# Expert choice sums its tokens with the choice as the stationary operand; key jobs, loads and sums of the distance attention in another order

## The reference, cut to what matters

```python
logits = jnp.einsum('bsd,de->bse', x, gate_w) + gate_b      # 32 experts
probs = jax.nn.softmax(logits, axis=-2)                     # over the tokens
vals, idx = top_k(probs, 8)                                 # 8 tokens of each expert and batch
merged = jnp.einsum('bked,bke->bed', tok, vals)             # their weighted sum, one row per expert
h = jax.nn.gelu(concat([merged, 1]) @ w1)                   # 257 x 1024 weights for each expert
o = concat([h, 1]) @ w2
out = scatter of o * vals to the chosen tokens
```

## Time and profile before

| | |
|---|---|
| median of 3 runs | 3237.09 us (3235.47 to 3243.7) |
| profiled execution: own time, span | 3209.46 us, 3207.6 us |
| PE busy | 2754.4 us, 86% of the span |
| DVE, ACT, POOL busy | 1873.4, 1721.7, 850.3 us |
| mean granted TensorE clock | 0.937 |
| expert choice, layer norm to the last sum | 1303.1 to 1528.5 us |
| opening of the layer 2 attention begins | 1529.3 us |
| opening of the layer 3 attention | 2319.5 to 2393.3 us |

### The profile page before, as it was taken

One profiled execution on the slowest core, in us unless ns is written; L12 is line 12 of the kernel. 1 busy time (PEld: TensorE's weight loads), 2 busy tenths in 40 slices (PEclk: granted clock), 3 DMA queues, 4 the chain that ended last, 5 costly groups with the idle time before them and its releaser, 6 DMA issues. The chain is left out here.

```text
span 3207.6 us, 46066 instructions
## 1 busy us (share of the span) xinstructions
PE 2754.4 (86%) x14806; PEld 1548.2 (48%) x14900; DVE 1873.4 (58%) x4757; ACT 1721.7 (54%) x2884; POOL 850.3 (27%) x957
## 2 busy tenths in 40 slices
PE   7899869959999999676699978999857888888887
PEld 3233249924444444432322247999633454444453
DVE  6677551155555555332688740111559999999953
ACT  3566522146555555111277732333149999999953
POOL 4101020030000000021300022000438888888840
PEclk8899989979999999788799999999978999999988
DMA  5111146510000000597212145999340000000011
GB/s 166 53 46 56 43 173 226 200 60 1 1 1 1 1 1 1 217 417 314 80 50 62 46 153 199 342 346 345 110 143 11 20 27 21 23 15 21 18 33 46
DMA packets 162662, 327.86 MB, mean 102 GB/s; under 512 B 29616, under 2 KB 129072, under 8 KB 139056
## 3 DMA queue, kind: packets, MB, share of 16 engines
q1 hardware_dynamic: 152976, 305.63, 27.4%
q0 software_dynamic: 4608, 12.59, 1.2%
q10 hardware_dynamic: 4896, 7.35, 0.7%
HBM read 276.08 MB, written 49.28 MB: 101 GB/s over the span
## 5 line engine op out<-in xcount | busy, mean ns | idle before, releaser
L3164 DVE TENSOR_TENSOR_SCAN L3x_behind<-L3x_first_exp,L3x_beside_scan 128x513 f32<-128x513 f32 x256 | 309.1, 1207 | 0.0
L3044 POOL TENSOR_TENSOR L3x_fade<-L3x_behind,L3x_apart 128x1024 f32<-128x1024 f32 x128 | 280.8, 2193 | 68.5 <-DVE L3x_behind L3164 44.9
L1334 ACT ACTIVATE L1x_probs<-L1x_scores,L1x_neg_max 128x512 f32<-128x512 f32 x256 | 173.5, 683 | 218.7 <-DVE L1x_neg_max L1386 218.7
L1386 DVE TENSOR_REDUCE L1x_neg_max<-L1x_scores 128x2 f32<-128x1024 f32 x128 | 156.5, 1223 | 144.0 <-PE L1x_scores L1234 144.0
L3082 ACT ACTIVATE L3x_first_exp<-L3x_scores,L3x_nm 128x512 f32<-128x512 f32 x256 | 231.6, 905 | 9.8 <-DVE L3x_nm L3156 9.7
L3110 ACT ACTIVATE L3x_probs_T<-L3x_probs_tp 128x512 f32<-128x512 f32 x256 | 207.0, 809 | 12.8 <-PE L3x_probs_tp L2972 12.8
L1667 ACT ACTIVATE L2f_hiddenT<-L2f_hidden_ps,L2f_b1s 128x128 f32<-128x128 f32 x320 | 99.8, 363 | 211.2 <-PE L2f_hidden_ps L1602 211.2
L806 DVE CUSTOM_DVE_ANT_0 L0x_masked_scores<-L0x_s,L0x_mask_q 128x512 f32<-128x512 f32 x256 | 167.0, 685 | 61.7 <-issue 55.8
L3090 ACT ACTIVATE L3x_fade<-L3x_fade,L3x_rl 128x512 f32<-128x512 f32 x256 | 200.5, 955 | 0.0
L801 DVE TENSOR_REDUCE L2x_neg_max<-L2x_s 128x1 f32<-128x512 f32 x256 | 164.6, 685 | 43.2 <-PE L2x_s L697 43.0
L3156 DVE TENSOR_REDUCE L3x_nm<-L3x_scores 128x1 f32<-128x512 f32 x256 | 172.6, 674 | 18.8 <-remote 17.1
(11 more groups left out here) (545 smaller groups left out, 6228.7 us busy)
## 6 DMA issues: line engine op xcount, KB each, us to landing
L2f_w1s<-in_L_w SPq DMA_DIRECT2D x40, 1024.0 KB, 7.7
L2f_w2s<-in_L_w SPq DMA_DIRECT2D x40, 1024.0 KB, 6.4
L1f_w1s<-in_L_w SPq DMA_DIRECT2D x32, 1024.0 KB, 15.4
L1f_w2s<-in_L_w SPq DMA_DIRECT2D x32, 1024.0 KB, 12.9
L0f_w1s<-in_L_w SPq DMA_DIRECT2D x16, 1024.0 KB, 6.1
L0f_w2s<-in_L_w SPq DMA_DIRECT2D x16, 1024.0 KB, 5.2
L0x_q_stack<-L0x_q_parts SPq DMA_DIRECT2D x96, 64.0 KB, 2.6
L0x_k_stack<-L0x_k_parts SPq DMA_DIRECT2D x96, 64.0 KB, 2.7
```

The source lines that it names most:

```text
L1334: nc.scalar.activation(p[:, n % 3, h, :], s[:, n % 2, h, :], ACT.Exp, bias=nmax[:, n % 4, h:h + 1], accum_out=den[:, n % 4, h:h + 1]).then ...
L3044: nc.gpsimd.tensor_tensor(fz[:, f:f + 2, :], bs[:, fb:fb + 2, 0:S], w, ALU.mult).then_inc(y_done, 1)
L3164: nc.vector.tensor_tensor_scan(bs[:, f, :], ex[:, t, :], beside[:, 0:1].to_broadcast([P, S + 1]), 0.0, ALU.add, ALU.bypass).then_inc(f_don ...
```

## The change

1. The sum of the chosen tokens has its operands exchanged: 32 columns of `selT` are stationary and 256 columns of the normed tokens move past, with the four batches in four groups of 32 output partitions. That makes 16 matmuls, a copy of the 128 x 256 result to SBUF, two transposes on PE and the two copies into `expert_tokens`.
2. The key jobs are spread anew. Groups 0 to 4 stay as they are. Group 5 has jobs 9 (between `up` and `turn`), 10 and 11, group 6 jobs 12, 13 and 14 in the same way, and group 7 only job 15, between `up` and `turn`. SP stores jobs 7, 8 and 9 in its turn 6, jobs 10, 11 and 12 in turn 7, and three at the end.
3. In an opening with keys made, ACT waits for the weights before its own loads, and a q job waits only for the two copies of its batch.
4. In the opening of layer 3, SP loads mask, gamma and distance at once after the weights. The sigmoids move to copies 1 to 4, the exponentials to copies 5 and 6 and jobs 1 and 3, the mask's terms and maxima ahead of the jobs on DVE, POOL's product ahead of its jobs, DVE's products to jobs 2, 4 and 6, and the sums of the values behind all jobs.

```diff
@@ norm_and_project, SP, PE
+                if beside:
+                    sp.wait_ge(*v_loaded)
+                    sp.wait_ge(*k_loaded)
+                    loads[3](sp)
...
-                    if j == max(NK - 1, 0):
+                    if j == max(NK - 1, 0) and not beside:
                         loads[3](sp)
...
-                pe.wait_ge(turn_free, NT // 2)
+                if not keys_made:
+                    pe.wait_ge(turn_free, NT // 2)
                 for j in range(NK, NJ):
+                    if keys_made:
+                        pe.wait_ge(turn_free, 2 * (j // MT + 1))
                     project(j)
...
+                if beside:
+                    value_sums(0)
+                    value_sums(2)
@@ norm_and_project, ACT
                 if keys_made:
+                    act.wait_ge(*v_loaded)
+                    act.wait_ge(*k_loaded)
                     loads[2](act)
...
-                    if beside and 3 <= i < 7:
-                        beside.sigmoid(act, i - 3)
-                if beside:
-                    beside.exponents(act, 0)
-                if keys_made:
-                    act.wait_ge(*k_loaded)
+                    if beside and 1 <= i < 5:
+                        beside.sigmoid(act, i - 1)
+                    if beside and i in (5, 6):
+                        beside.exponents(act, i - 5)
...
-                    if beside and j in (NK, NK + 2, NK + 4):
-                        beside.exponents(act, 1 + (j - NK) // 2)
+                    if beside and j in (NK + 1, NK + 3):
+                        beside.exponents(act, 2 + (j - NK) // 2)
@@ norm_and_project, DVE, POOL
                 if beside:
                     beside.gamma_low(dve)
+                    prepare[1](dve, mask_made)
+                    mask_maxima()
...
-                    if beside and j in (NK + 2, NK + 5):
-                        beside.product(dve, 1 + (j - NK) // 4)
+                    if beside and j in (NK + 2, NK + 4, NK + 6):
+                        beside.product(dve, (j - NK) // 2)
...
                 if beside:
-                    beside.product(dve, 3)
                     beside.gamma_end(dve)
+                    read_sums(0)
+                    read_sums(2)
...
+                if beside:
+                    beside.pool_product(pool, 0)
                 for j in range(NK, NJ):
@@ expert_choice, the choice
-                    for b in range(B):
-                        for k in range(KD):
-                            for t in range(TB):
-                                last = nc.tensor.matmul(mps[:, k, b * E:(b + 1) * E],
-                                                        c.xn[:, b * TB + t, k * P:(k + 1) * P],
-                                                        selT[:, t, b * E:(b + 1) * E], start=(t == 0),
-                                                        stop=(t == TB - 1))
+                    for t in range(TB):
+                        for b in range(B):
+                            last = nc.tensor.matmul(mps[b * E:(b + 1) * E, 0:D], selT[:, t, b * E:(b + 1) * E],
+                                                    c.xn[:, b * TB + t, :], start=(t == 0), stop=(t == TB - 1))
                     last.then_inc(merged_done, 1)
+                    pe.wait_ge(merged_out, 1)
+                    for k in range(KD):
+                        last = nc.tensor.transpose(mtp[:, k, 0:P], merged[:, k * P:(k + 1) * P], c.ident[:])
+                    last.then_inc(merged_turned, 1)
...
                     dve.wait_ge(merged_done, 1)
+                    nc.vector.tensor_copy(merged[:], mps[:, 0:D]).then_inc(merged_out, 1)
+                    dve.wait_ge(merged_turned, 1)
@@ expert_choice, the key jobs
+            between, first, second = ([None] * 5 + [9, 12, 15], [None, 1, 3, 5, 7, 10, 13, None],
+                                      [0, 2, 4, 6, 8, 11, 14, None])
...
                         move(g - 1)
-                        for j in range(max(2 * g - 5, 0), 2 * g - 3):
-                            later.store(sp, j)
+                        if g >= 2:
+                            for j in (first[g - 2], second[g - 2], between[g - 1]):
+                                if j is not None:
+                                    later.store(sp, j)
@@ DistanceWeights
+    def constant_loads(self, sp):
+        sp.dma_start(self.gam[:], self.dram["gammas"].partition_broadcast(P)).then_inc(self.const_loaded, 16)
+        sp.dma_start(self.distance[:], self.dram["distance"].rearrange("(t p) k -> p t k", p=P)
+                     ).then_inc(self.const_loaded, 16)
```

More of the change, by code:

```diff
@@ L355, in _ @@
                         rotate(j - 1)
-                    if masked and j in (NK + 3, NK + 5):
+                    if masked and j in (NK + 3, NK + 5) and not beside:
                         value_sums(j - NK - 3)
@@ L2197, in _ @@
                         move(g - 1)
-                        for j in range(max(2 * g - 5, 0), 2 * g - 3):
-                            later.store(sp, j)
+                        if g >= 2:
+                            for j in (first[g - 2], second[g - 2], between[g - 1]):
+                                if j is not None:
+                                    later.store(sp, j)
                     move(G - 1)
-                    for j in range(2 * G - 5, len(later.jobs)):
+                    for j in (first[G - 2], second[G - 2], between[G - 1]):
                         later.store(sp, j)
@@ L2287, in _ @@
                         if g:
-                            later.leading(act, second_of(g - 1))
-                        if g == G - 1:
-                            later.take(act, 2 * g - 1)
+                            later.leading(act, second[g - 1])
+                        if between[g] is not None:
+                            later.take(act, between[g])
                         act.wait_ge(b_done, g + 1)
@@ L2295, in _ @@
                                              ).then_inc(g_done, 1)
-                        if g:
-                            later.take(act, first_of(g))
-                            later.leading(act, first_of(g))
-                        later.take(act, second_of(g))
+                        if first[g] is not None:
+                            later.take(act, first[g])
+                            later.leading(act, first[g])
+                        if second[g] is not None:
+                            later.take(act, second[g])
                 @block.vector
@@ L2321, in _ @@
                         if g:
-                            later.split(dve, second_of(g - 1))
-                        if g == G - 1:
-                            later.split(dve, 2 * g - 1)
+                            later.split(dve, second[g - 1])
+                        if between[g] is not None:
+                            later.split(dve, between[g])
                         dve.wait_ge(o_done, g + 1)
@@ L2327, in _ @@
                                                 ).then_inc(o_staged, 1)
[L2328 to L2331 removed]
+                        if first[g] is not None:
+                            later.turn_by_angle(dve, first[g])
+                            later.split(dve, first[g])
                     for t in range(NT):
```

58 lines of the change are left out of this document (26 added, 32 removed).

## The result

| | before | after |
|---|---|---|
| median of 16 runs | 3236.74 us (3233.12 to 3243.7) | 3230.57 us (3228.08 to 3235.7) |
| profiled execution: own time, span | 3209.46, 3207.6 us | 3229.67, 3227.9 us |
| mean granted TensorE clock | 0.937 | 0.935 |

A forecast was written before the change was run, and what follows sets the result against it. Each stretch had its own limit: a PE chain, then weight loads in expert choice, and detours in layer 3's opening. -3.0 + 1.1 - 0.6 - 17.4 = -19.9 us off the 3237.1 median gave 3217.2, range 3208 to 3228.

The forecast's parts named there:

- the upper bound of +8: Expert choice, key jobs: the worst expected, if both groups run the DMA dry; the forecast was +1.1 us.
- Gelu and `down(5)` come 4 us later, which the 4 MB of `w1(6)` in flight hide: Expert choice, group 5: job 9 ahead of the Gelu delays it 4 us, hidden by the weight transfer.
- The slack is just used up: Expert choice, group 6: `w2(7)` is issued 8.5 us late, leaving the DMA idle for about 0.7 us.
- moved the landing by 1.7 us: Expert choice, group 7: the store job 14 waits for lands at 1502.0, not 1500.3, so `down(7)` ends 3.7 us later.
- the bound that was named for it: Opening of layer 2, q jobs: -0.6 us if the splits behind pass it on, otherwise 0.
- the bound of -12: Opening of layer 3: least gain, if `pdiff` holds ACT 3 us more and products and evictions fall apart; forecast -17.4.
- in all 6.3 MB flow, at the 386 GB/s, from 2324.7: Opening of layer 3: loads of both queues flow until 2341.0, the first two batches landing near 2330.7 and 2336.1.
- `pdiff` landing after 2342: Opening of layer 3: one of the named signs that would make the forecast wrong; the last batches were expected by 2341.5.
- E: Rival, chance 0.1: both expert groups run the DMA dry for 4 us each, layer 3's opening gains 11; 3232 us.
- C: Rival, chance 0.2: layer 3's opening gains only 11 us, since ACT and not the order limits it; 3224 us.
- F: Rival, chance 0.02: slower, the DMA queue starves in all of expert groups 5 to 7; 3247 us.
- 2 us at most for an early POOL product: Opening of layer 3: a POOL product ahead of the first split could cost DVE's first cast up to 2 us once.

The follow-up runs named there:

- e3: The kernel before with the exchanged operands of the chosen-token sum alone; 3230.38 us, ratio to before 0.9982.
- e1: The changed kernel with the key jobs and their stores spread as before; 3220.49 us, ratio to before 0.9952.
- e4: The kernel before with the new openings of layers 2 and 3 alone; 3220.86 us, ratio to before 0.996.
- e2: The changed kernel, with SP storing the two jobs of group g-2 ahead of its wait for `down(g-1)`; 3218.82 us, ratio to before 0.995.
- f1: The early-store kernel e2 with ACT issuing `pdiff` at once, its wait for weights behind its own loads; one run, 3212.37 us, layer 3 opening 59.1 us.
- f2: The early-store kernel e2 with SP issuing mask, gamma and distance only when the second `pdiff` batch has landed; one run, layer 3 opening 58.8 us.
- f3: The early-store kernel e2 with the mask's load, terms and maxima placed as before the change; one run, layer 3 opening 69.9 us.
- g1: The changed kernel with both repairs, early stores and `pdiff` at once (f1 again, measured five times); 3179.08 us, ratio to before 0.993.
- g3: The changed kernel with key jobs spread as before and `pdiff` issued at once; 3182.35 us, ratio to before 0.994.
- g2: The changed kernel with `pdiff` issued at once as its only edit; 3193.0 us, ratio to before 0.9972.
- f4: The early-store kernel e2 with the sums of the values at their old places, after jobs 3 and 5; one run, layer 3 opening 66.7 us.

## Why the prediction was wrong, by its own steps

Sum of the stages: -2.8 (part 1, e3) + 8.9 (part 2, after against e1) + 0.4 (part 3) - 11.8 (part 4) = -5.3 us, against -5.5 by the ratio. The forecast was -19.9. That the two agree so well is chance: parts 1 and 2 taken together are +7.1 in the table and not +6.1, and the attention behind is 1.3 us shorter.

- **Part 1, -3.0 forecast, -2.8 measured.** Right, with its steps: 3.64 us against 3.7 for the sum, 0.42 for the copy as read from another row, and all but 3 us of the 9 hidden by the transfer, during which the DMA moved 401 to 459 GB/s without a gap (before it fell to 49 and then 0).
- **Part 2, +1.1 forecast, +8.9 measured**, just above the upper bound of +8. The mechanism was the one described: jobs 11 and 14 wait for stores of jobs 7 and 10 that SP issues behind `w2`, and the copy of `h` is queued behind them (14.48 and 13.56 us; "some 13"). The sizes failed, in three terms. With part 1's 3.0 us taken off the forecast, and all times counted from the layer norm, `down(7)` ended 9.0 us late.
  - The first and largest failure is the step "Gelu and `down(5)` come 4 us later, which the 4 MB of `w1(6)` in flight hide". In group 5 I took PE to be warm behind the wait of job 9. It stood 3.56 us, the clock was 0.50, and `project` and `down(5)` took (3.78 - 1.98) + (4.88 - 3.66) = 3.0 us more. `w2(6)` was issued 160.1 us after the layer norm where e1 has 152.4: 7.7 us later, not 4. The DMA ran dry (2.6 us) and then thin (1.7 us), and job 11 was released 4.4 us late (177.2; e1 has a wait for the same store end at 172.8, where the forecast put it). What the low clock adds is read from the rows; no run has the wait without it.
  - In group 6 the cold `project` took 3.78 us, not 3.1: `w2(7)` was issued another 0.6 us late. "The slack is just used up" failed with this: the DMA was dry for 3.8 us where I had 0.7.
  - In group 7 it took 16.1 us from the issue of `w2(7)` (1489.71) to the release of job 14 (1505.85), and I had 12.1. I had moved the landing by 1.7 us from where it was before. `w2(7)` alone fits in that: at 386 GB/s its 4 MB would be through at 1501.6 in the forecast's clock. What I did not have is what three stores in one turn do, at the 290 GB/s of those 6 us: the store of job 10 was the first of them, but landed only when the DMA had all but emptied (186 GB/s from 1505 to 1506, 32 behind).
  - The last group's tail gained as forecast: DVE's first sum follows `stage` (1515.91) by 4.6 us, where I had 4.5 and before has 7.1.
- **Part 3, -0.6 forecast, about 0 measured** (63.7 to 64.1 us; 62.7 in e4), the bound that was named for it. The first q job did start 0.6 us earlier (27.4 us after the layer norm, and 28.0 before), but the first scores did not come earlier. In e2, f1, f2, f3 and g1 this opening takes 61.1 to 62.3 us: there the granted clock stays at 1.00 from 8 us after the layer norm on, in the other kernels only from 12 to 14 us on, and q starts at 25.4. So 2.6 us of what e2 gained on after lie in this stage, and not where its edit is meant to work.
- **Part 4, -17.4 forecast, -11.8 measured**, just past the bound of -12. The values start at T+3.7, as forecast. Then the term "in all 6.3 MB flow, at the 386 GB/s, from 2324.7" fails: both issues wait for the weights, ACT's comes at T+5.6 and not at T+4.3, and the first windows show 150, 29 and 256 GB/s. Sigmoid 1 runs at T+20.7 where I had its batch landed at T+16.6. The sign of being wrong that was named for this, `pdiff` landing after 2342 (T+22.5), came: the last sigmoid waited for its batch until T+26.1. f1 and f2 show that this is nearly the whole of the shortfall of 5.6 us: without the late `pdiff` the attention begins at T+56.4 and T+56.1 (T+57.0 to 57.6 in g1 to g3), against 56.4 forecast. Two smaller errors cancel in that: the first eviction is then 1.8 us earlier than forecast, and from it to the attention it takes 27.3 us where I had 25.5, of which 1.2 us lie between the last store and the attention (4.6 and not 3.4).
- **The rivals.** E (both groups run dry for 4 us each, the opening gains 11; 0.1) is what happened: 2.6 and 3.8 us, and 11.8. I treated its two halves as one rare mishap. They have separate causes: e1 has the short opening without the dry stretches, and e2 repairs the one and g2 the other. Each should have had its own chance. C (the opening gains only 11, for ACT is its limit; 0.2) had the right size for part 4 and the wrong reason: in f1 ACT does the same work and the opening takes 4.9 us less.
- Slips in its sums, none of which decides anything: from its own figures the DMA would have stood idle 0.1 us and not 0.7 (1490.7 against 1490.6), a store and four loads are 2.48 us and not 2.45, and no working is given for F's 3247.
- The Trainium skill, "SBUF — State Buffer", section "Who interferes with whom", was weighed with 2 us at most for an early POOL product. It says that beside a VectorE instruction in a 2-port mode whichever of VectorE and GpSimd issues first gets the shared ports for the whole instruction and the other is fully blocked, and it counts `tensor_scalar` among the operations that can enter such a mode. The trace agrees, though it doesn't show the mode: DVE's tiny L492 stood 4.12 us and ended at 2389.48, with the product that began at 2384.94 and took 4.52. In e1, e2 and e4 the same instruction took 0.17 us. What it cost is not shown apart: their first q evictions are alike (T+34.1 to 34.5), but their attention begins at T+60.8 to 61.3 and not 62.1, so it is about 1 us at most. In f1 and g1 to g3 it took 3.5 us, in the shortest openings.

## What to carry to other kernels

Where a job moves ahead of work that feeds a transfer, follow the buffer it will wait for back to the place in the queue where its store is issued: SP's two lines of e2 were worth more than the whole new spread cost. Where a new wait leaves PE standing (behind 3.56 us of it the clock was 0.50 here), price what comes behind it at the low clock as well, and ask whether a stream of weights has that much left in flight. And an issue that waits for an earlier transfer leaves the DMA empty between the two; put the wait behind the issue, and let the transfer that is needed first have the DMA alone.

## What the runs showed that was not expected

Behind PE's standstill of 3.56 us the granted clock was 0.50, and the same `project` took 3.78 us where it takes 1.98 at 1.00.

In the opening of layer 3 the DMA fell to 302 and 222 GB/s in two windows of 2 us while all its loads had been issued (151 GB/s in the 2 us from T+12). e1, e2, e4 and f4 have the same fall, to 156 to 167 GB/s. In f3, without the mask, the windows at the same place show none of it:

```profile
2353.00:2355.00 2.00, 2.00 (x13) 1.74 (x12) 1.44 (x4) 0.59 (x1) 1.26 (x2) 1.00 1.03 375
2355.00:2357.00 2.00, 2.00 (x13) 1.82 (x12) 1.32 (x5) 1.41 (x2) 0.92 (x2) 1.00 1.05 381
2357.00:2359.00 2.00, 2.00 (x13) 1.77 (x12) 1.33 (x5) 1.99 (x2) 1.57 (x2) 1.00 1.05 400
```

But the mask alone doesn't make it: f1 and g1 to g3 load it too, and have no such fall (here f1, from T+11.3):

```profile
2353.00:2355.00 2.00, 2.00 (x13) 1.77 (x12) 1.32 (x4) 1.16 (x2) 0.86 (x1) 1.00 1.04 386
```

All kernels with the fall issue `pdiff` and the mask, gamma and distance at the same moment, at T+4.9 to 5.6; in f1 and g1 to g3 `pdiff` goes out at T+1.0 and the mask at T+7.8 to 8.4. Why is open. One of ACT's four issues took 2.9 us in after (0.5 for the others), but so it did before (2.5 us) and in g1 (2.3 us), where nothing fell.

The feed-forward of layer 2, which no kernel here changes, took 442 to 445 us in the profiled executions of before, g1, g2 and g3, and 474 to 478 in the others. The first use of its sorted rows, in g1 (layer norm at 1866.1) and in f1 (1865.1):

```profile
L1606 PE MATMUL L2f_rows_tp<-identity,L2f_rows x80: 272/273/327, 1956.3 to 2240.4; 128*128 128x128 f32 x80
```

```profile
L1606 PE MATMUL L2f_rows_tp<-identity,L2f_rows x80: 272/273/328, 1978.7 to 2263.1; 128*128 128x128 f32 x80
```

It is 90.2 us behind the layer norm in the one and 113.6 in the other, and the 284 us of matmuls that follow are equal. The rest comes behind them, between the first gather and the end: 49.1 us in g1 (from 2258.9), 60.1 in f1 (from 2281.6). The cause stays open. It is why a sum over stages was made. The profiled execution of before, 27 us below the median, has the short form of this stage and the median most likely the long one; the forecast took its gain off the median, so this did not add to its error.
